# Decoder layer on one core: the V products of self attention cut into two column halves and moved between the score products

## What is computed

```
B, N, C = x.shape                       # 1, 2048, 256;  H, D = 16, 16
q, k, v = qkv[0], qkv[1], qkv[2]        # q and k after RoPE
attn = jnp.einsum('bhqd,bhkd->bhqk', q, k) * SCALE
diff = jnp.where(pos[None, :] - pos[:, None] > 0, 0.0, pos[None, :] - pos[:, None])
attn = attn + diff[None, :, :] * slopes[:, None, None] * MAX_BIAS
w = jax.nn.softmax(attn, axis=-1)
out = jnp.einsum('bhqk,bhkd->bhqd', w, v)
```

## Time and profile before

| what | us |
|---|---|
| median of 3 runs | 2022.4 (2009.4 to 2033.74) |
| the profiled execution | 2020.26 |
| its span, first to last instruction | 2018.5 |
| TensorE busy in the span | 1795.3 (89%) |
| VectorE busy | 1396.5 (69%) |
| ScalarE busy | 1177.2 (58%) |
| GpSimd busy | 350.9 (17%) |

### The profile page before, as it was taken

The page is one execution under the profiler, slowest core; times in us unless marked ns, Lnnn a source line. Parts: engine busy times, 40 slices in busy tenths (PEclk is TensorE's granted clock), DMA queues, the critical chain, the costliest instruction groups (busy, mean ns, idle before and its releaser), DMA issues.

```text
span 2018.5 us, 30282 instructions
## 1 busy us (share of the span) xinstructions
PE 1795.3 (89%) x10422; PEld 935.9 (46%) x10422; DVE 1396.5 (69%) x2807; ACT 1177.2 (58%) x2401; POOL 350.9 (17%) x561
## 2 busy tenths in 40 slices
PE   5908899999999999998589999999999885999993
PEld 2504333333333333333344444444444254999993
DVE  6506799999999999952488999999999144111113
ACT  1201277777777777776307777878777741333333
POOL 6104022222222222202000000000000002333331
PEclk9956599999999999999758999999999875999997
DMA  6421000000100000000202010100102123777773
GB/s 239 168 88 45 2 26 26 27 26 30 36 33 30 26 27 26 26 2 23 106 18 78 28 35 29 33 31 29 36 23 84 42 71 128 194 202 202 200 201 100
DMA packets 72608, 140.14 MB, mean 69 GB/s; under 512 B 14140, under 2 KB 47309, under 8 KB 70237
## 3 DMA queue, kind: packets, MB, share of 16 engines
q1 hardware_dynamic: 64746, 127.84, 18.8%
q0 software_dynamic: 7712, 10.37, 3.1%
HBM read 109.07 MB, written 28.45 MB: 68 GB/s over the span
## 4 chain that ended last, share of the span: by engine, by line
PE 70%; DVE 13%; ACT 6%; issue 4%; DMA 3%; SPq 3%; POOL 0%; POOLq 0%; DVEq 0%; ACTq 0%
PE banks L936 21%; PE banks L923 21%; PE banks L885 8%; PE banks L1107 7%; PE banks L1117 7%; ACT XT L1174 3%; DVE wset L1353 3%; DVE skip L1353 2%; PE banks L839 2%; DVE CM L1349 2%; DVE CM L1344 2%; ACT late L1174 2%; PE banks L843 1%; PE banks L896 1%; DMA kxD<-parts 1%
## 5 line engine op out<-in xcount | busy, mean ns | idle before, releaser
L1174 ACT ACTIVATE XT<-banks 128x512 f32<-128x512 f32 x1240 | 658.4, 600 | 288.8 <-PE banks L923 198.3
L885 PE MATMUL banks<-oper 52*128 52x512 f32 (+1 forms) x2048 | 734.2, 453 | 39.9 <-DVE CM L1353 14.9
L923 PE MATMUL banks<-oper 54*128 54x512 f32 x1856 | 691.8, 457 | 34.2 <-POOL oper L718 10.5
L923 PEld LDWEIGHTS banks<-oper 54*128 54x128 f32 x1856 | 310.0, 188 | 537.5 <-ACT XT L1174 311.6
L1344 DVE TENSOR_REDUCE CM<-banks 128x1 f32<-128x402 f32 x1024 | 512.1, 566 | 18.6 <-PE banks L885 7.4
L885 PEld LDWEIGHTS banks<-oper 52*128 52x128 f32 x2048 | 361.6, 196 | 149.6 <-DVE CM L1353 69.0
L1174 ACT ACTIVATE late<-banks 128x512 f32<-128x512 f32 x616 | 327.9, 600 | 93.7 <-PE banks L923 79.2
L936 PE MATMUL banks<-XT,VS 128*32 128x512 f32 x2480 | 339.8, 621 | 1.3 <-ACT XT L1174 0.7
L1251 ACT ACTIVATE HID<-banks,b1E 128x128 f32<-128x128 f32 x312 | 85.4, 382 | 182.9 <-DMA b1E<-in_b1T_dram 165.2
L1518 DVE TENSOR_TENSOR YB<-banks,b2E 128x256 f32<-128x256 f32 x39 | 16.6, 425 | 252.3 <-PE banks L1117 252.3
L936 PE MATMUL banks<-late,VS 128*32 128x512 f32 x1232 | 168.4, 619 | 0.3
(11 more groups left out here) (210 smaller groups left out, 1447.7 us busy)
## 6 DMA issues: line engine op xcount, KB each, us to landing
W<-in_w1T_dram SPq DMA_DIRECT2D x39, 1024.0 KB
oper<-kD SPq DMA_DIRECT2D x32, 256.0 KB
W2R<-in_w2T_dram SPq DMA_DIRECT2D x8, 1024.0 KB, 7.6
oper<-kxD SPq DMA_DIRECT2D x32, 208.0 KB
b2E<-in_b_dram SPq DMA_DIRECT2D x39, 128.0 KB
qD<-parts SPq DMA_DIRECT2D x8, 512.0 KB, 2.7
kD<-parts SPq DMA_DIRECT2D x8, 512.0 KB, 2.7
oper<-kD SPq DMA_DIRECT2D x32, 128.0 KB
```

The source lines that it names most:

```text
L885: mm = pe.matmul(slot[:, n * QB:n * QB + ch], QO[64 * g:64 * g + M_ROWS, c2, col:col + P], KO[64 * g:64 * g + M_ROWS, c2, k0:k0 + ch], sta ...
L923: pe.matmul(bank, KO[64 * g:64 * g + S_ROWS, c, b * P:(b + 1) * P], QO[64 * g:64 * g + S_ROWS, c, q0:q0 + QB], start=True, stop=True).then ...
L1174: act.activation(PT[(c * plan.nu + u) % PRING], S[(c * plan.nu + u) % SBANKS], ACT.Exp).then_inc(A.exps, 1)
```

## The change

The plan of self attention is given `vparts` 2 and another sequence. Cross attention keeps its own.

```
-SELF = Plan(TT, QB, True, False, 1, {2: "m S0 m S1 m S2 m V0 m S3"})
+SELF = Plan(TT, QB, True, False, 2, {2: "m S0 m S1 V0 m S2 m V1 S3"})
```

## The result

The changed kernel took 2178.7 us (median of 4 runs, 2145.5 to 2204.5) against 2015.9 before: a ratio of 1.069, 95% interval 1.052 to 1.087. Run again beside the kernel before it took 2181.8 against 2006.0, ratio 1.088 (1.084 to 1.092). The ratio 1.069 compares the two shorter of the four executions of the change, 2145.5 and 2171.2 us, with the kernel before (the medians alone give 1.081), and the profiled execution, 2186.2 us, is one of the two longer ones. It is slower, as forecast, by about twice what was forecast: 2107 was said, with 2072 to 2140 as the range.

The account below looks back on a forecast made before the run. The loop exponential, S2, V batch, S3 (2.61 us per tile) was taken as the bound, VectorE a near second. 84.6 + 2.7 - 3 = +84 us on 2022.4 gave 2106, with half clock 2107; range 2072 to 2140.

Parts of the forecast that it names:

- The loop: Self attention's key tile: exponential, V0, third max product with S2 and fourth one, V1, S3, together 2.97 us against 2.61.
- A half batch: V0 or V1 in a self-attention tile: 0.56 us each, bounds 0.50 to 0.99, where a whole batch costs 0.99.
- the changes of mode: Changing between score and V products drains TensorE: about 0.1 us lost on the way in and 0.1 out; two more per tile.
- The growth of 0.36 per tile: Each of 235 self-attention tiles with max items goes from 2.61 to 2.97 us, 84.6 us in all.
- VectorE is the real bound: Self-attention rival: V0's wait costs nothing, tile stays 2.61 us, sum and shift waits leave S3's path; 2008 us, 4%.
- the extra changes cost nothing: Self-attention rival: half batches cost 0.50 each and 0.66 stays between; +0.24 us on 235 tiles, 2075 us, 9%.
- a half batch costs nearly a whole one: Self-attention rival: at 0.99 us per half the loop is 3.83, 2330 us; at a midpoint of 0.75, 2205; 4%.
- The special tiles: Tiles 1, 3, 4 and 12 of a head: 2.2 us extra against 2.4 before, -3 us over 14 heads.
- Half clock at the start: Head 0, at half clock until 250 us: four or five tiles pay some 0.2 us more each, raising 2106 to 2107.
- The sum: Whole program: 84.6 + 2.7 - 3 = +84 us, giving 2106 on the median, 2107 with head 0's half clock.
- The clock falls: Rival: TensorE idles in every tile, so half of self attention runs at half clock; 2235 us, 2%.
- the 21 tiles without max items: End of self attention: each goes from 2.61 to 2.74 us, 2.7 us in all.

Follow-up runs that it names:

- both halves together: Kernel before with the V batch in two halves, both ahead of S3 where the whole batch stood: 2011.5 us, ratio 1.003.
- S1 twice: Score product S1 computed twice into its bank: in the changed kernel 2672.7 us, ratio 1.336; in the kernel before 2003.8 us, ratio 0.998.
- the exponential in four: Kernel before with S3's exponential done in four pieces of 128 columns: 2046.7 us, ratio 1.021.
- the items behind S3: Kernel before with four m in the sequence instead of five, so the sum and shift items fall behind S3: 2016.4 us, ratio 1.004.
- the old order at the ends: Changed kernel with the order of the kernel before, both halves ahead of S3, in heads 0, 14 and 15: 2093.1 us, ratio 1.042.
- old ends with S1 twice: Changed kernel with the old order in heads 0, 14 and 15, and S1 computed twice in heads 1 to 13: 2101.6 us, ratio 1.048.
- batch behind S3: Kernel before with the whole V batch moved behind S3: 2106.0 us, ratio 1.051.
- whole batch early: Kernel before with the whole V batch moved between S1 and S2: 2081.9 us, ratio 1.038.
- third max product ahead of V0: Changed kernel with the third max product moved back ahead of V0: 2122.6 us, ratio 1.061.
- the fp32 product in the change: Changed kernel with one fp32 product of the identity with itself put into S1's bank ahead of S1: 2840.6 us, ratio 1.416.

## Why the prediction was wrong

**The loop: right.** Its five steps were forecast as 0.65, 0.56, 0.66, 0.56, 0.54 and are 0.65, 0.57, 0.66, 0.57, 0.54. A half batch of 0.57 is by 0.07 more than half of 0.99, as the changes of mode asked; with both halves together that excess is gone. The growth of 0.36 per tile was measured as 0.37. The rivals "VectorE is the real bound", "the extra changes cost nothing" and "a half batch costs nearly a whole one" all fall with the tile of 2.98 us. (The second of them had "the third max product hides" in its name, but its +0.24 kept the full 0.66 between the halves; with a hidden third max product it would have been nearly nothing.)

**The special tiles: nearly right.** Above 2.98 they cost 0.58 (tile 1; 0.5 said), 0.73 (tile 3; 0.7), 0.56 (tile 4; 0.5) and 0.84 (tile 12; 0.5). Together that is 2.7 us where 2.2 was said: 0.5 per head, 7 us in all. Most of it is tile 12. The prediction let S0 there wait for GpSimd alone. The trace of the change shows a later wait:

```profile
727.51 0.18 PEld L923 LDWEIGHTS banks<-oper 54*128 54x128 f32 x1 [0.41 <-ACT late L1174]
...
727.93 0.14 PEld L892 LDWEIGHTS banks<-idf,SHW 128*128 128x128 f32 x1 [0.24 <-issue]
728.16 0.29 POOL L718 CAST oper<-zeros 4x128 fp32r<-4x128 f32 x1 [5.44 <-PE banks L923]
...
728.63 0.18 PEld L885 LDWEIGHTS banks<-oper 52*128 52x128 f32 x1 [0.56 <-DVE CM L1353]
...
729.53 0.16 PEld L936 LDWEIGHTS banks<-late,VS 128*32 128x32 f32 x8 [0.37 <-issue]
```

GpSimd is done at 728.45, but the shift's transpose has taken a slot, and the next max product, ahead of S0, waits for VectorE until 728.63. V0 comes 2.02 after S3 instead of 1.71.

**Half clock at the start: too small.** "Four or five of its tiles pay more for the two changes, some 0.2 each" took the half-clock stretch to end at 250 us whatever runs in it. A half-clock tile of the change is 4.75 us against 4.07 before, 0.68 more, where the 0.37 of full clock and 0.2 would make 0.57, and the stretch lasted to 258 and to 353 us in two traces.

**The clock: this is the step that failed.** The sum held 1 us for half clock, the few tiles at the start, and nothing else; measured are 87. The rival "The clock falls" had 2% and a price of 2235. I set it aside because "the last head has four score products and one V batch in 2.61 us, less than any changed tile has in 2.97, and keeps clock 1.00". That compared two unlike tiles by the amount of work, and took one stretch that holds the clock as proof for all with more work. The stretch was no firm ground even by itself: in two later traces the last head, in the old order, lost the clock with tiles of 2.6 us. I also asked only whether the clock would fall in mid heads, and never what it does in the change's own last head, whose tiles were to go from 2.61 to 2.74 us with nothing added: that stretch fell in both traces of the change and stayed at half clock to its end, 4.23 us a tile. For the 21 tiles without max items I had put down 2.7 us; in the traces they cost about 34 more than at full clock's 2.74 (21 x 1.5 = 32, and the special ones). The price was too small as well: it took 1.0 us more for a half-clock tile, the old order's 4.0 less the new order's 2.97, where a changed tile goes from 2.98 to 4.75, 1.77 more. In the first trace the mid-head stretch of 133 us, which the second did not have, added about 51 (heads 10 to 12 took 59.8, 81.1 and 61.1 against 50.4), the start 3. Together with the order's 95 that is the 182.

**What the runs say of the cause.** Shown: the growth by the order alone is 81 us for 13 heads, and the rest goes with the time at half clock. Shown too, by S1 twice in two places: the same order and the same products can stay at half clock for over 1300 us when they begin there, and hold full clock through 13 heads when they begin there.

The half-clock stretch at the start of self attention ended at 250 us (the kernel before, the halves together, the exponential in four), 249 (the items behind S3, the old order at the ends), 241 (S1 twice before) and 235 (old ends with S1 twice). The 249 and the 235 have the same head 0, so some 14 us are chance. With another order in head 0 it ended at 237 (batch behind S3), 238 (whole batch early) and 239 (third max product ahead of V0), at 258 and 353 (the change), and not at all (S1 twice and the fp32 product in the change). A half-clock tile is 4.07 us before, 4.75 in the change, 5.17 and 5.77 in the last two. That looks as if longer tiles kept the clock down, but the variant with the third max product ahead of V0 speaks against length alone: its first half-clock tile took 5.14 us, the change's 5.24, and its clock rose right after.

The falls lie in two places. One is the stretch without max items, at the end of self attention. There the clock fell in every trace of a variant that has longer tiles there and had the full clock before. But it also fell with tiles of 2.6 us: at 979 and 1020 us in the last head of the two runs with the old order at the ends, at 942 us in the last tile of the items behind S3, and for 3 us in the halves together. The other is tile 12 of a mid head, the longest of the head (the change, both traces, and the whole batch early).

Still open: why the change fell in a mid head for 133 us in one trace, for 3 us in the second, and not in the third-max variant whose tiles are as long; and what TensorE's work must be for the clock to rise. One trace per variant doesn't settle it, and no run varied the V products' share alone.

No variant is faster than the kernel before. The nearest is the kernel before with S1 twice, which is the same within its interval.

## What to carry to other kernels

Find the loop that closes on itself (here exponential, S2, V batch, S3) and write down what each moved instruction adds to it; here work that fits in front of a wait's release was free (0.23 us into a wait of 0.28), and work moved behind it came into every round. For the change that sum was right to 0.01 us. In two of the other variants it was not, by 0.26 us and by 0.35 or more, because another loop closed first: the slot of the max items, and S0 with its bias. So add up the next loops as well. Then ask of every stretch, the first and the last above all, whether it begins or ends at half clock: a loop that is 14% longer here cost 7 to 9% of the whole program, about half of it by half clock, and a stretch at half clock may keep itself there. And price a stretch that holds the clock now by what it will look like after the change, not by another that seems thinner.

## What the hardware showed that I had not expected

More work for TensorE can be nearly free or very dear. One more score product per tile gave 2003.8 us on the old order (ratio 0.998). On the change it cost some 10 us (2101.6 against 2093.1) when heads 1 to 13 began at full clock, and 491 us (2672.7 against 2181.8) when they began at half clock. In that state TensorE was busy 99% for 1347 us and the granted clock stayed at 0.50. A busy TensorE is thus no sign that the clock will rise: the Trainium skill, "TensorE: Matmul & The Clock Gate", section "What's actually happening", says that activity releases the throttle, and by what these windows show the busy share of the profile isn't that activity. The falls did not come behind long idle stretches either: in the first trace TensorE's longest idle time between 258 and 780 us, where it first fell, is 0.8 us, and 1.2 us ahead of the fall at 1029.

Four short activations of 128 columns in place of one of 512 lengthened the loop by 0.19 us, less than the 0.5 that I had taken from starts 0.25 apart in the experts' stage.
